# Decoder layer on one core: two tiles instead of four share each set of wide products

## The reference

```python
x = _layernorm(x + _L0_attn_ref(x, ...))     # S4D: long convolution by FFT, skip term, its own layernorm
x = _layernorm(x + _L0_xattn_ref(x, ctx, ctx, ...))  # 16 heads of 16, 77 keys, softmax
x = _layernorm(x + _L0_ffn_ref(x, ...))
# the last one:
sim = einsum(q, keys); sc, ix = top_k(sim, 8)      # product keys: 64 x 64 (1024 experts used), 4 heads
scores, pk = top_k(all pair sums, 8)
w = silu(h . down_embed[idx]) * softmax(scores)    # 4 heads x 8 experts for each token
out = silu(h @ Wg + bg) * (h @ Wu + bu) @ Wd + bd + sum(w * up_embed[idx])
```

## Time and profile before

| | us |
|---|---|
| median of 3 runs | 709.79 |
| profiled execution, whole time | 716.18 |
| profiled execution, span | 714.3 |
| TensorE busy | 620.8 (87%) |
| VectorE busy | 517.7 (72%) |
| ScalarE busy | 405.0 (57%) |
| POOL busy | 288.8 (40%) |

### The profile page before, as it was taken

How to read it: one execution, slowest core, us unless ns; L and a number is a source line. 1 busy time by engine, 2 the same in 40 slices (tenths; PEclk the granted TensorE clock), 3 DMA queues, 4 the chain that set the end, 5 groups by cost and what they waited for, 6 DMA issues and landing times.

```text
span 714.3 us, 9686 instructions
## 1 busy us (share of the span) xinstructions
PE 620.8 (87%) x3120; PEld 413.6 (58%) x3120; DVE 517.7 (72%) x1052; ACT 405.0 (57%) x593; POOL 288.8 (40%) x341
## 2 busy tenths in 40 slices
PE   5773967878675868999999999999999999999896
PEld 2432556767563645455478565477665469554485
DVE  7999998813244788588767778785778787677783
ACT  4961652231114335598675578767478866477660
POOL 0009456413422236633235625226543334544361
PEclk9876988998979557799999999999999999999999
DMA  8953030183807000000000000000000000000000
GB/s 263 375 192 80 1 121 3 55 174 73 191 11 295 1 0 1 0 0 1 1 0 1 9 15 1 8 2 1 8 8 9 8 1 1 8 16 7 0 8 22
DMA packets 20366, 35.24 MB, mean 49 GB/s; under 512 B 7644, under 2 KB 14301, under 8 KB 18589
## 3 DMA queue, kind: packets, MB, share of 16 engines
q1 hardware_dynamic: 15933, 30.44, 14.0%
q10 hardware_dynamic: 4384, 4.20, 2.1%
HBM read 22.92 MB, written 10.65 MB: 47 GB/s over the span
## 4 chain that ended last, share of the span: by engine, by line
PE 59%; DVE 30%; issue 5%; ACT 5%; POOL 1%; DMA 0%; SPq 0%; DVEq 0%; ACTq 0%; POOLq 0%
PE bank L779 19%; PE bank L869 7%; PE bank L874 7%; PE bank L824 4%; DVE arena L1345 3%; PE bank L846 3%; DVE arena L1346 3%; DVE arena L1344 3%; PE bank L801 3%; PE bank L836 3%; PE bank L810 2%; DVE stats L1383 2%; PE bank L692 2%; DVE arena L1474 1%; PE bank L861 1%
## 5 line engine op out<-in xcount | busy, mean ns | idle before, releaser
L1185 POOL TENSOR_TENSOR arena<-arena 128x1024 f32<-128x1024 f32 x64 | 126.0, 1968 | 157.0 <-ACT arena L1073 155.9
L779 PE MATMUL bank<-arena 128*128 128x512 f32 x384 | 174.5, 596 | 5.9 <-issue 3.6
L779 PEld LDWEIGHTS bank<-arena 128*128 128x128 f32 x384 | 69.8, 190 | 83.7 <-issue 76.6
L1073 ACT ACTIVATE arena<-arena 128x1024 f32<-128x1024 f32 x64 | 73.5, 1149 | 7.5 <-DVE arena L1472 3.2
L1075 ACT ACTIVATE arena<-arena 128x1024 f32<-128x1024 f32 x64 | 73.5, 1149 | 2.1
L1474 DVE SCALAR_TENSOR_TENSOR arena<-arena 128x1024 f32<-128x1024 f32 x48 | 64.0, 1333 | 1.7
L869 PE MATMUL bank<-arena 128*128 128x256 f32 x256 | 58.4, 381 | 2.9 <-DVE arena L1496 1.4
L963 ACT COPY arena<-bank 128x512 f32<-128x512 f32 (+1 forms) x64 | 34.1, 533 | 43.7 <-PE bank L771 30.0
L874 PE MATMUL bank<-arena 128*128 128x256 f32 x256 | 57.9, 379 | 0.0
L1158 POOL TENSOR_SCALAR arena<-mv 128x1 f32<-128x1 f32 (+1 forms) x40 | 15.0, 375 | 104.8 <-DVE mv L1384 103.4
L869 PEld LDWEIGHTS bank<-arena 128*128 128x128 f32 x256 | 47.4, 190 | 10.7 <-issue 3.3
(11 more groups left out here) (191 smaller groups left out, 1191.5 us busy)
## 6 DMA issues: line engine op xcount, KB each, us to landing
scr_x<-arena SPq DMA_DIRECT2D x16, 256.0 KB, 2.9
arena<-scr_x SPq DMA_DIRECT2D x2, 2048.0 KB, 14.2
arena<-scr_z SPq DMA_DIRECT2D x32, 128.0 KB, 4.7
scr_z<-arena ACTq DMA_DIRECT2D x14, 256.0 KB, 2.5
tok<-in_x SPq DMA_DIRECT2D x8, 256.0 KB, 5.3
out<-tok SPq DMA_DIRECT2D x16, 128.0 KB, 1.7
arena<-in_fmat SPq DMA_DIRECT2D x1, 1600.0 KB, 7.9
arena<-in_imat SPq DMA_DIRECT2D x1, 1600.0 KB, 8.4
```

The lines of the kernel that those rows point to most:

```text
L779: ins = mm(bk[:, :], w[:, k, P * m:P * m + P], src[:, k, :], start=(k == 0), stop=(k == KC - 1))
L1073: fn(ebuf[m % 2], sxb[m % 2], ACT.Prelu, bias=negt[:, n % 2, h:h + 1], alpha=FAR).then_inc(s_ranked, 1)
L1185: tt(sxb[m % 2], sim[:, n % 2, h, 0:XR].unsqueeze(2).broadcast_to((P, XR, NKEYS)), sim[:, n % 2, FH + h, :].unsqueeze(1).broadcast_to((P, ...
```

## The change

`SUPER` is 2, so W is 256. A wide unit (`wide`) fills one bank with two chunks of 128 weight columns for 256 tokens (`PAIR` = 2). There are four `expert` and four `inner` steps for a set in place of eight, and one `query` step. ScalarE and VectorE have biases per chunk, so `query`, `inner`'s gate and tanh, and `hid` are issued once per chunk; `expert`'s passes stay whole. `turn1` and `turn2` are one step each for the set. `silg`, `hid`, `x2T` and `qT` have two buffers; `rw` has two tiles. Waits for a free buffer look back two sets. `PLACE` and `LAG` have new numbers.

```diff
-SUPER = 4
+SUPER = 2
+PAIR = 2
...
-         "project": (1.4,), "project_last": (0.934,), "turn1": (-0.087, 0.0423), "query": (0.245, 0.2676),
-         "turn2": (-0.001, 0.0646), "sim": (0.379,), "sim_first": (0.031,), "best": (0.432,), "best_first": (0.207,),
+         "project": (1.389,), "project_last": (0.934,), "turn1": (-0.05, 0.0422), "query": (0.179, 0.2677),
+         "turn2": (0.097, 0.2001), "sim": (0.263,), "sim_first": (0.171,), "best": (0.432,), "best_first": (0.3,),
...
         if i == 0:
-            return [("expert", f, c) for c in range(6)]
-        if i == 1:
-            return [("expert", f, 6), ("expert", f, 7)] + [("inner", f, c) for c in range(4)]
-        if i == 2:
-            return [("inner", f, c) for c in range(4, 8)] + [("spread", r, 0), ("spread", r, 1)]
-        return [("outer", r), ("spread", r + 1, 0), ("spread", r + 1, 1), ("outer", r + 1),
-                ("spread", r + 2, 0), ("spread", r + 2, 1), ("outer", r + 2)]
+            return [("expert", f, c) for c in range(EC // PAIR)] + [("inner", f, c) for c in range(FC // PAIR // 2)]
+        return [("inner", f, c) for c in range(FC // PAIR // 2, FC // PAIR)] + [("spread", r, 0), ("spread", r, 1), ("outer", r)]
...
                 bk = w_unit(key)
-                for k in range(KC):
-                    ins = mm(bk[:, :], w[:, k, P * m:P * m + P], src[:, k, :], start=(k == 0), stop=(k == KC - 1))
+                for j in range(PAIR):
+                    at = P * (PAIR * m + j)
+                    for k in range(KC):
+                        ins = mm(bk[:, W * j:W * j + W], w[:, k, at:at + P], src[:, k, :], start=(k == 0),
+                                 stop=(k == KC - 1), skip_group_check=True)
                 ins.then_inc(s_wmm, 1)
...
                 elif kind == "turn2":
-                    pe.wait_ge(s_x2, SUPER * n + 2 * step[2] + 2)
+                    pe.wait_ge(s_x2, SUPER * n + SUPER)
...
-                    fn(gate[:, m % 3, :], src, ACT.Identity, scale=0.5, bias=pcol[:, 4 + c:5 + c])
-                    tanh_of(step, src, bias=pcol[:, 4 + c:5 + c])
+                    for j in range(PAIR):
+                        fn(gate[:, m % 3, W * j:W * j + W], src[:, W * j:W * j + W], ACT.Identity, scale=0.5, bias=bias[j])
+                    tanh_of(step, src, bias)
...
-                    if n and c == 0:
-                        dve.wait_ge(s_7mm, SUPER * n)
-                    stt(hid[:, c, :], w_bank(u)[:, :], pcol[:, 4 + FC + c:5 + FC + c], gate[:, m % 3, :], ALU.add,
-                        ALU.mult).then_inc(s_wdve, 1)
+                    if n >= 2 and c == 0:
+                        dve.wait_ge(s_7mm, SUPER * (n - 1))
+                    for j in range(PAIR):
+                        ch, at = PAIR * c + j, slice(W * j, W * j + W)
+                        ins = stt(hid[n % 2][:, ch, :], w_bank(u)[:, at], pcol[:, 4 + FC + ch:5 + FC + ch],
+                                  gate[:, m % 3, at], ALU.add, ALU.mult)
+                    ins.then_inc(s_wdve, 1)
```

More of the change, by code:

```diff
@@ L90 @@
[L90 to L96, removed]
+PLACE = {"probs": (0.166, 0.2584, 0.4394), "score": (0.273, 0.697), "attend": (0.471,), "turno": (0.821,),
+         "project": (1.389,), "project_last": (0.934,), "turn1": (-0.05, 0.0422), "query": (0.179, 0.2677),
+         "turn2": (0.097, 0.2001), "sim": (0.263,), "sim_first": (0.171,), "best": (0.432,), "best_first": (0.3,),
+         "pair": (0.283, 0.3895, 0.7906, 0.8002), "total": (0.875,), "first": (-0.1,), "sums": (-0.51,),
+         "exps": (-0.131,), "late": (-0.011, 0.0074, 0.427),
+         "conv": (-2.338, -1.7123, -1.4986, -1.4219, -1.3322, -1.2945, -1.1768, -0.9651),
+         "ln": (-1.672, -1.4043, 0.3144, 1.2221, 1.9374, 2.369, 3.0302, 3.1379),
+         "ln_steps": (-0.336, -0.234, 0.127, 0.013, 0.361), "sines": (-3.002, -2.884), "tables": (-0.426,),
+         "taps": (0.776,), "x_second": (-0.756, 0.506), "skip": (0.382,), "k_first": (5.072, 0.1, 9.0, 0.065),
+         "simw": (-2.0,), "x_bias": (2.891, 0.086), "values": (2.778,), "diagonal": (-1.625,),
+         "k_second": (5.484, 0.287, 9.065, 0.116), "spectra": (5.6, 0.264, 9.07, 0.1),
+         "inverse": (6.097, 0.357, 9.272, 0.133), "products": (0.2, 1.0, -0.083, 0.97, 0.0, 0.8, -0.08, 0.97),
+         "probs_alone": (0.016, 0.0783, 0.4716), "score_alone": (0.367, 0.711), "attend_alone": (0.536,),
+         "turno_alone": (0.734,), "project_alone": (1.12,), "dev2": (0.037,), "norm2": (0.093,), "dev3": (0.454,),
+         "norm3": (0.779,)}
@@ new lines @@
+LAG = {("dve", "score"): 0.14, ("act", "score"): 0.206, ("act", "best"): 0.054, ("dve", "attend"): 0.046,
+       ("dve", "expert"): 0.099, ("dve", "inner"): 0.102, ("dve", "outer"): 0.141, ("dve", "spread"): 0.104,
+       ("dve", "project"): 0.018, ("act", "norm1"): -0.003, ("act", "norm3"): 0.334, ("dve", "pair"): 0.128,
+       ("dve", "ln"): -0.555, ("dve", "residual"): -0.098, ("pool", "turn1"): 0.507, ("pool", "turn2"): -0.115,
+       ("pool", "dev1"): 0.053, ("act", "diagonal"): 0.473, ("act", "dev2"): 0.38, ("act", "probs"): 0.035,
+       ("pool", "best"): -0.311, ("dve", "total"): 0.102, ("pool", "pair"): -0.061, ("dve", "turn1"): -0.01,
+       ("act", "first"): 0.034, ("act", "products"): 0.022, ("pool", "turno"): -0.001, ("pool", "dev3"): -0.036,
+       ("pool", "skip"): -0.009}
@@ L125, in queries @@
         for kind in ("turn1", "query"):
-            for j in range(2):
-                put(start, kind, s, j, j=j)
+            put(start, kind, s, 0)
     def normed(at, tl, k):
@@ L171, in plan @@
         if i == 0:
-            for j in range(2):
-                put(start, "turn2", s, j, j=j)
+            put(start, "turn2", s, 0)
             put(start, "sim", tl, key="sim_first")
```

96 lines of the change are left out of this document (47 added, 49 removed).

## The result

| | before | after |
|---|---|---|
| median, us | 710.2 (708.4 to 716.6) | 750.7 (744.6 to 751.9) |
| profiled execution / span, us | 716.2 / 714.3 | 751.9 / 749.9 |
| first keys product, us | 289.1 | 256.7 |
| from the first to the last set's keys product, us | 324.5 (12 tiles) | 433.4 (14 tiles) |
| from the last keys product to the end, us | 100.8 (four tiles) | 59.8 (two tiles) |

After takes 1.0517 times as long [1.0465, 1.057]. It is slower, as I forecast, but by 40.5 us where I had 16.5, and outside my range of 706 to 745. Executions more than 1.5% above the fastest of their kernel count as slow, and all ratios here leave them out, while the medians in us take in every execution.

A forecast was written before the change was run, and what follows sets the result against it. TensorE's own queue was taken to bound the kernel from 300 us on. Lead 261, periods 413.8 and tail 56 summed to 730.8 us against a 714.3 span, +16.5: median 726, own range 717 to 735, 8 in 10 706 to 745.

The forecast's parts named there:

- VectorE's crowding: First period: residual and ln steps of later convolution tiles, some 12 us, of which 5 reach TensorE; bounds 0 and 12.
- Lead: Start to first keys product: 261 us in place of 289.1, so -28 us; bounds -31 and -24.
- Half-width products: Wide units on TensorE as four products of 256 columns: counted as 0; bounds 0 and 2 us.
- Passes: ScalarE's and VectorE's passes issued per 256 columns fit beside TensorE: counted as 0; bounds 0 to 8 us.
- Handover: From a set's last project to its keys product: 3.6 us idle per two-tile period; bounds 1.9 and 5.
- Second wait: Behind project of a set's first tile, before the next score product: 1.2 us TensorE idle; bounds 0 and 2.
- Clean period: Undisturbed period of two tiles: 111.2 / 2 - 0.95 + 3.6 + 1.2 = 59.4 us, seven in all.
- Clock: Rival, 0.15: TensorE's clock drops at each of seven handovers, 2.3 us lost each, +16, 742 us.
- First period: Between the first two sets' keys products: -3.2 us for no late outer, +5 for VectorE's queue.
- Median: Span difference of +16.5 us put on the median of before, 709.8: forecast 726 us.
- Tail: From the last set's keys product to the end, two tiles: 56 us; bounds 53 and 62.
- Lead wins: Rival, 0.23: handovers cost 1.9 us a period, no second wait or crowding; sum 706, 702 at the median.

The follow-up runs named there:

- a_score: The changed kernel with only VectorE's score step earlier, ahead of the first pair step (lag 0.14 to 0.136): 747.7 us, 1.0501 of before.
- b_passes: The kernel before, with inner's gate, tanh and hid passes issued as two of 256 columns: 718.0 us, 1.0087 of before.
- b_half: The kernel before, with each wide product of 512 columns issued as two of 256: 711.7 us, 0.9997 of before.
- a_nowait: The changed kernel, turn2 transposing a constant array, norm wait moved to POOL, norm2 later, total earlier; feed-forward input is other data: 726.1 us, 1.0188 of before.
- a_free: a_nowait, with VectorE's score step also ahead of the first two pair steps of a set's second tile: 713.4 us, 1.0037 of before.
- a_spare: The changed kernel with 256-column products that nobody reads placed where TensorE would wait, no wait shortened: 740.6 us, 1.0398 of before.
- a_first: The changed kernel with ScalarE's passes for heads 0 and 1 of the first tile cut to 64 of 1024 columns: 748.5 us, 1.0548 of before.
- a_fill: The changed kernel with the late outer of a set's second tile moved right ahead of turn2: 777.6 us, 1.0914 of before.
- a_swap: The changed kernel with project of a set's last tile ahead of the outer of the previous set's first tile: 776.0 us, 1.0889 of before.
- a_split: The changed kernel with turn2 one step per tile and the first tile's keys product right behind the last project: 733.8 us, 1.0303 of before.

## Why the prediction went wrong

The direction was right, and so was the mechanism that I put the loss on: each handover between sets of two has over 3 us idle, there are seven, and the lead gains some 30 us. Two terms of the sum failed. The half clock behind the waits stood in it with 0, as a rival that excludes the forecast; it takes 9.6 us of the later periods, and by my estimate 4 more of the first and 2 of the tail. And the first period, with 5 us for VectorE's crowding, was mis-sized. Term by term, from the span of the profiled execution (730.8 predicted, 749.9 measured):

| term | predicted | measured | difference |
|---|---|---|---|
| lead to the first keys product | 261 | 256.7 | -4.3 |
| clean period of two tiles, seven times | 59.4 | 59.9 | +3.4 |
| first period's own excess | -3.2 + 5 | 8.4 | +6.6 |
| half clock in the other periods | 0 (a rival) | 9.6 | +9.6 |
| tail | 56 | 59.8 | +3.8 |

- *Lead, 261.* Right. Its 4.3 us less are no more than leads differ by: 252.3 us in a_score, 256.7 in after; 289.1 in before, 284.2 in b_passes, whose edit doesn't touch it.
- *Half-width products: 0.* Right (b_half).
- *Passes: 0 of 0 to 8.* Mis-sized: 6 us in before (b_passes). What they cost in after was not tried by itself; they may be part of the clean period below.
- *Handover, 3.6 us.* Right in size, 3.3 (my own 5.2 less 1.7 is 3.5), and it is real time: a_nowait gets 24.6 us back, some 16 of them in the seven periods.
- *Second wait, 1.2 us.* Right in the trace; its price was more, since the clock falls behind it. Taking it away from a_nowait gave 12.7 us, 1.8 a period.
- *Clean period, 59.4.* Right in sum, from two errors that cancel. TensorE was busy 55.9 us of the 59.9, where I had 54.65 of work, and idle 4.0, where I had 4.8. a_free agrees: without waits 56.8. Of the 1.2 us more of work 0.25 was there before (109.80 us busy in the 111.23 of four tiles, so 54.9 for two), and b_half has 0.12 more than that; the rest was not broken down.
- *Clock: 0 in the sum, the first step that failed.* I gave it as a rival, a case that excludes the forecast. It adds to it: 9.6 us in the table's own row, and a_spare gives 10 us back. I also placed it at the handover alone. It falls there in some sets (the keys products of 2.4 to 2.9 us), but at 494 us it follows the second wait, and the handover of the same period, from 506 us, leaves it at 1.00.
- *First period: the second.* I let 5 of VectorE's 12 us reach TensorE. The period is 68.3 us, 8.4 above the clean one where I had 1.8, and a_spare (67.4) and a_free (66.7) keep it. Two things are in the 8.4. TensorE is idle for 12.1 us there and for 4.0 in the clean period. And it is busy as long as there (56.1 and 55.9 us) with 32 records less, an outer of 7 us, since its granted clock is 0.90: some 7 us of half clock, of which before's first period had some 3 (4 us less busy than its clean one for the same 32 records), so that they were in my -3.2. These are estimates; by them 4 of the 6.6 us are the clock again.
- *What TensorE waits for there.* In after 6.5 us for ScalarE, whose exponentials stand ahead of the copy that attend needs, and 5.4 for VectorE; a_first takes most of the first away, and VectorE has the same time again. Both queues are late, and clearing one is no gain. VectorE's steps for the convolution's norms cost more than their rows said, by some 4 us, in four passes beside POOL's sums (rows of after; the row at 294.56 is the price alone, and the pair at 264.57 takes 1.01 us at 293.51; POOL's pair ahead of these rows runs from 262.48 to 266.40):

```profile
264.57 2.63 DVE L1417 SCALAR_TENSOR_TENSOR arena<-arena,mv,rows 128x256 f32<-128x256 f32 x2
...
266.83 2.13 POOL L1195 TENSOR_TENSOR arena<-arena 128x1024 f32<-128x1024 f32 x1 [0.43 <-ACT arena L1083]
267.23 2.00 DVE L1421 SCALAR_TENSOR_TENSOR tok<-arena,rstd,tok 128x256 f32<-128x256 f32 x1
...
269.19 1.90 POOL L1195 TENSOR_TENSOR arena<-arena 128x1024 f32<-128x1024 f32 x1 [0.24 <-ACT arena L1083]
...
269.95 1.42 DVE L1421 SCALAR_TENSOR_TENSOR tok<-arena,rstd,tok 128x256 f32<-128x256 f32 x1
...
294.56 0.48 DVE L1421 SCALAR_TENSOR_TENSOR tok<-arena,rstd,tok 128x256 f32<-128x256 f32 x1
```

Each of the single passes ends 0.3 us behind a pass of POOL. In a_first a pass over 32 columns is caught too: 1.90 us, where at 276.58 the same takes 0.19, and it ends at 263.54 where POOL's pair of passes ends at 263.50 (in after that pass took 0.19 us, at 262.46). The Trainium skill (SBUF — State Buffer, Who interferes with whom) says that a VectorE pass with two inputs in SBUF and a GpSimd pass that reads SBUF exclude each other; these rows agree. How much of the first period's excess this lock makes isn't shown: no run took POOL's sums out of it.
- *Median.* I put +16.5 on the median of before. Its profiled execution was 6.4 us above that median, after's is 1.2 above its own: 5 of the 24 us by which I was off.
- *Tail, 56.* 3.8 us more; the last set's first keys product, 3.80 us for 1.98, is half of it, by the clock again. In a_spare the tail is 57.9.
- *"Lead wins" was worse than I wrote it.* I gave 706 for a kernel with the waits of the old one; a_free, with almost none, has a span of 712.2; its first period is 66.7 us, where that sum had 3.2 less than a clean one.

## What to carry to other kernels

Splitting a set multiplies its handovers. Count the latencies between the last step of one set and the first of the next, and ask which long block covers each; moving a block fills one gap and opens the one that it covered (a_fill, a_swap); what gained here was a piece of the step behind the gap (a_split). A wait can have a second price at TensorE's clock; it adds to the forecast and belongs in the sum. When a change makes two stages overlap, price each pass by rows in which the other engine of the pair was at work.

## What the hardware showed that I had not expected

A wait of 1.2 us can cost more than one of 3.3: in after the clock fell to 0.50 for six us behind the short one, which ended a stretch with 1.84 us of work in three, and stayed at 1.00 over the handover that came next. Spare products in the gaps, read by nobody, made the kernel 10 us faster (1.0398 [1.0344, 1.0452] of before, where after is 1.0517 [1.0465, 1.057]). And a VectorE pass of 0.19 us can take ten times as long beside a GpSimd pass of 2 us, in before too (1.90 us at 297.54, beside POOL's sums from 295.45 to 301.37).
